# Four column tiles where sums or values run alone, and another order of the preparation

## The chip, the core and the metric

One core of one Trainium2 chip runs the whole program. The metric is the device time of one execution in microseconds (us), the median of several. The engines are TensorE (PE; its weight loads are PEld), VectorE (DVE), ScalarE (ACT), GpSimd (POOL) and SyncE (SP), which here issues every transfer. Each works through its own instructions in program order and waits on semaphores.

## The reference

Two layers of a gated decoder block on `x` and `ctx_1024`, both (8, 512, 256) in fp32. The first attention is the one that matters here:

```python
scores = jnp.einsum('bhqd,bhkd->bhqk', q, k) / math.sqrt(D_K)      # 16 heads, D_K = 16, S = 512
scores = jax.nn.softmax(scores, axis=-1)
col_sum = jnp.sum(scores, axis=2)                                  # how much each key is looked at
_, idx = jax.lax.top_k(col_sum, int(S * 0.9))                      # 460 of 512 keys stay
mask = zeros.at[..., idx].set(1.0)
out = jnp.einsum('bhqk,bhkd->bhqd', scores * mask[:, :, None, :], v)
```

Each part is added to the stream as `x + tanh(gate) * part(...)`. Behind this attention stand its output product, a feed-forward of width 704 with weights and inputs rounded to FP4 in blocks of 16, a second attention with a layer norm (without a softmax, so it becomes one 256x256 matrix per batch), and a linear layer rounded to 8 bits.

## The kernel before, in words

The work has three stages which share one program order per engine.

**Preparation** (`prepare`, `project`). SP loads weights and inputs in the order of `first`, `second` and `first_batch`. `project` makes for each batch the projections q, k, v (steps `Q0`, `Q1`, `K0`, `K1`, `V0`, `V1`), the transposes of the normalised x (`XT0`, `XT1`), and the matrix of the second attention (`GRAM`, `X1`, `RB`, `KV`, `MM`, `ROW`). `SEQ` lists these steps. The first 16 (`AHEAD`), up to `KV` of batch 1, run before the attention begins; the later ones are cut into pieces and put between the steps of the attention (`at_turn`, `ends_at`). q and k go out to HBM (`store_q`, `store_k`) and come back in another layout (`load` in `attend`, called `load_heads` in `run`). `stats(b)` takes the sums for the layer norm of x of batch b on DVE, `normal` applies it. `Fp4Weights` rounds the feed-forward's weights: `load` on SP, `maxima`, `scales`, `over` and `round` on DVE, `magnitude` on ACT, `split` on POOL, at the steps z of `LARGEST_AT` and `HALF_AT`.

**Attention** (`attend`). A unit u is half of the heads of a batch, 16 units, each of 16 steps z, 256 steps in all. In step z PE makes scores for two heads into `ps_a` (L1275), DVE takes their row maxima (`nmax`, L1356), ACT the exponentials into `ea` (L1442). `column_sums` (L1311) multiplies `ea` by the reciprocals of the row sums and adds up the keys' sums in `ps_s`; from its partitions 0 to 63 DVE ranks the keys of a unit (`rank_step`, from L1384) and marks the dropped ones. `LAG` = 42 steps later the scores are made again, with the mask and the softmax's shift as further rows of the product, into `ps_b`, ACT makes `prob` (L1458, and in the last steps L1455 head by head), and `values` (L1325) adds up the outputs in partitions 64 to 127 of `ps_s`, which DVE copies to `att` after every 8 steps (`leave`, L1408). Sums and values are products with 32 output columns, so one takes a strip of 32 columns of PE's array. A step has two heads of sums (strips 0 and 1) and two heads of values (strips 2 and 3):

```python
            for h in range(2):
                e.matmul(ps_s[32 * h:32 * h + 32, :], ...)            # column_sums, L1311
            for h in range(2):
                o = SUMS + 32 * h
                e.matmul(ps_s[o:o + 32, :], ...)                      # values, L1325
```

The trace counts each fp32 product as two matmuls. Values begin at z = 46 and end at z = 301, sums run from z = 4 to z = 259: before and after that one of the two is alone, on two strips.

**Feed** (`feed`). 16 units of 256 tokens go through output product (`first_product`, L1701), FP4 feed-forward (`gate_or_up`, L1728), second attention and 8-bit layer. Its first turns stand between the last 46 steps of the attention: `first_product` after steps 262, 268 and 284, `x_T` after 273 and 286, `gate_or_up` after the steps 275 to 282 and 288 to 295.

Of the kernel before, what the change touches and what calls it, by code (L numbers as in the profile page):

```python
# [9 lines left out]
F16 = mybir.dt.float16  # L10
# [65 lines left out]
CONST, CLEARED, ZEROED = 6, 8, 10  # L76
# [129 lines left out]
def prepare(m, a, w, ey, tiles, bank):  # L206
# [11 lines left out]
    def sync(e):  # L218
# [16 lines left out]
        def first():  # L235
# [26 lines left out]
    def gpsimd(e):  # L262
# [11 lines left out]
        e.tensor_copy(w.ident16[:, :], w.ident[:, :]).then_inc(w.s_set, 1)  # L274

# [26 lines left out]
    def vector(e):  # L302
# [46 lines left out]
        return bias_scale, bias_operand, round_w8, gated, scale_w8  # L349
# [7 lines left out]
class Fp4Weights:  # L357
# [37 lines left out]
    def load(self, e):  # L395
        a, w = self.a, self.w
        e.wait_ge(w.s_set, CLEARED)
        for n, name in enumerate(["L0_ffn_w_gate", "L0_ffn_w_up"]):
            e.dma_start(self.gn[:, n * FC:n * FC + FC - 1],
                        a[name][0:(FC - 1) * P].rearrange("(c p) i -> p c i", p=P)).then_inc(self.s_load, 16)  # L400
            e.dma_start(self.gn[0:FL, n * FC + FC - 1], a[name][(FC - 1) * P:F]).then_inc(self.s_load, 16)
        e.dma_start(self.dn[:, :, :], a["L0_ffn_w_down"].rearrange("(c p) i -> p c i", p=P)).then_inc(self.s_load, 16)
# [121 lines left out]
LARGEST_AT, HALF_AT = (0, 9, 18), (2, 6, 11, 15, 20, 24)  # L524


def project(m, a, w, ey, scr, bank, fp4):
# [100 lines left out]
    def sync(e):  # L628
# [245 lines left out]
    def vector(e):  # L874
# [32 lines left out]
        def fill(s):  # L907
# [186 lines left out]
def attend(m, w, scr, tiles, fp4):  # L1094
# [22 lines left out]

    APART = ALL_Z - LAG
# [9 lines left out]
    rank, top = m.sb("rank", [SUMS, T]), m.sb("top", [SUMS, 8])  # L1128
    drop = m.two("drop", [SUMS, T], F16)
# [34 lines left out]
    def sync(e):  # L1164
# [107 lines left out]
    def tensor(e):  # L1272
# [29 lines left out]
        def column_sums(g, k):  # L1302
# [1240 lines left out]
```

## Time and profile before

| | |
|---|---|
| median of 3 runs | 1188.7 us (1186.08 to 1189.09) |
| the profiled execution | 1184.63 us, its span 1182.9 us |
| PE busy | 1075.4 us, 91% of the span |
| DVE busy | 993.3 us, 84% |
| ACT busy | 905.6 us, 77% |
| POOL busy | 303.1 us, 26% |
| mean granted clock of PE | 0.971 |

Busy shares are means over the three stages and have to be read stage by stage: the preparation fills the first 45 us, the attention goes on until about 790 us, the feed alone until the end. The profiled execution took 1.7 us outside its span, and its own time is 0.3% under the median of the runs.

### The profile page before, as it was taken

To read this page: it belongs to the slowest core of one execution; us is meant where nothing else is said; L and a number is where in the kernel's file an instruction comes from. 1 tells how busy PE (TensorE), PEld (TensorE's weight loads), DVE (VectorE), ACT (ScalarE), POOL (GpSimd) and SP (SyncE) were. 2 spreads that over 40 slices of the span, in tenths; PEclk is the share of its full clock that TensorE was granted. 3 is DMA by queue.
4 is the path that set the end of the run, shared out by engine and by line. 5 is a ranking of instruction groups with operands and counts; after the bars stand their busy time and mean duration, and the time that the engine had idled before them with its cause. 6 is when DMAs were issued, how large, how long until landed. Compare 5 with 4: busy or idle time off the path is not lost.

```text
span 1182.9 us, 17878 instructions
## 1 busy us (share of the span) xinstructions
PE 1075.4 (91%) x5580; PEld 479.5 (41%) x5580; DVE 993.3 (84%) x1906; ACT 905.6 (77%) x2044; POOL 303.1 (26%) x473
## 2 busy tenths in 40 slices
PE   7697999999999999999998779999999999999975
PEld 4232232222232222232232113336677777777653
DVE  7599999789889889888789867357999999999965
ACT  4366799999989999999898985764677667667634
POOL 7264431221222222312211212002222212222212
PEclk9798999999999999999999989999999999999985
DMA  9712133134313222331322011001012111210001
GB/s 301 163 65 66 41 91 96 45 87 99 70 50 108 76 70 64 100 86 38 86 65 48 21 51 55 10 14 58 27 37 63 43 39 37 63 45 19 21 17 36
DMA packets 75966, 75.98 MB, mean 64 GB/s; under 512 B 11560, under 2 KB 67680, under 8 KB 75872
## 3 DMA queue, kind: packets, MB, share of 16 engines
q1 hardware_dynamic: 75872, 74.84, 23.0%
q8 instruction: 45, 0.74, 0.3%
q14 instruction: 49, 0.40, 0.1%
HBM read 47.02 MB, written 27.28 MB: 63 GB/s over the span
## 4 chain that ended last, share of the span: by engine, by line
PE 55%; ACT 20%; DVE 16%; issue 7%; DMA 1%; SPq 1%; POOL 0%; DVEq 0%; ACTq 0%
PE ps_a L1728 13%; ACT ea L1442 10%; PE ps_b L1686 8%; PE ps_s L1311 8%; ACT prob L1458 6%; DVE nmax L1356 6%; PE ps_s L1325 4%; PE ps_s L1686 3%; PE ps_b L1275 3%; PE ps_f L1701 2%; PE ps_f L831 2%; PE ps_a L1737 2%; PE ps_a L1275 2%; PE ps_f L802 2%; PE ps_f L1762 1%
## 5 line engine op out<-in xcount | busy, mean ns | idle before, releaser
L1442 ACT ACTIVATE ea<-ps_a,nmax 128x512 f32<-128x512 f32 x512 | 357.1, 726 | 65.9 <-DVE nmax L1356 64.6
L1356 DVE TENSOR_REDUCE nmax<-ps_a 128x2 f32<-128x1024 f32 x256 | 311.4, 1217 | 48.3 <-PE ps_a L1275 45.9
L1311 PE MATMUL ps_s<-ea,rz 128*32 128x512 f32 x1024 | 275.5, 617 | 19.9 <-DVE rank L1384 12.6
L1325 PE MATMUL ps_s<-prob,v_pad 128*32 128x512 f32 x1024 | 271.8, 610 | 4.3 <-DVE att L1408 3.5
L1458 ACT ACTIVATE prob<-ps_b 128x1024 f32<-128x1024 f32 x214 | 230.1, 1075 | 4.6 <-PE ps_b L1275 3.8
L1728 PE MATMUL ps_a<-wgu,xT 128*128 128x352 f32 x512 | 165.4, 463 | 3.3 <-ACT xT L1891 2.1
L1275 PE MATMUL ps_b<-q_st,k_st 52*128 52x512 f16 x512 | 102.8, 384 | 28.7 <-ACT prob L1458 26.5
L1442 ACT ACTIVATION_READ_ACCUMULATOR ea<-ps_a,nmax 128x1 f32 x512 | 125.2, 245 | 0.0
L1728 PEld LDWEIGHTS ps_a<-wgu,xT 128*128 128x128 f32 x512 | 92.4, 190 | 57.9 <-issue 14.5
L1275 PE MATMUL ps_a<-k_st,q_st 48*128 48x512 f16 x512 | 100.9, 390 | 5.5 <-ACT ea L1442 5.3
L1903 ACT ACTIVATE ea<-ps_a 128x352 f32<-128x352 f32 x128 | 59.5, 466 | 59.2 <-PE ps_a L1728 59.0
L1686 PE MATMUL ps_b<-wdn,hT 128*128 128x256 f32 (+1 forms) x384 | 94.9, 392 | 0.0
L1275 PEld LDWEIGHTS ps_a<-k_st,q_st 48*128 48x128 f16 x512 | 24.7, 93 | 147.3 <-ACT ea L1442 78.3
L1311 PEld LDWEIGHTS ps_s<-ea,rz 128*32 128x32 f32 x1024 | 37.6, 109 | 104.6 <-issue 91.5
L1686 PEld LDWEIGHTS ps_b<-wdn,hT 128*128 128x128 f32 (+1 forms) x384 | 67.6, 189 | 22.5 <-issue 15.9
L1395 DVE MATCH_REPLACE8 rank<-top,rank 64x512 f32<-64x512 f32 x112 | 74.8, 668 | 0.1
L1389 DVE MAX8 top<-rank 64x8 f32<-64x512 f32 x112 | 73.5, 656 | 0.2
L1455 ACT ACTIVATE prob<-ps_b 128x512 f32<-128x512 f32 x84 | 45.6, 597 | 32.4 <-PE ps_b L1275 32.3
L1275 PEld LDWEIGHTS ps_b<-q_st,k_st 52*128 52x128 f16 x512 | 26.5, 94 | 84.0 <-ACT prob L1458 46.5
L1629 POOL TENSOR_TENSOR x_in<-x_in,rows 128x512 f32<-128x512 f32 x16 | 20.4, 1272 | 118.8 <-DVE r L2067 103.6
L1325 PEld LDWEIGHTS ps_s<-prob,v_pad 128*32 128x32 f32 x1024 | 38.1, 108 | 28.6 <-issue 25.1
L1629 POOL TENSOR_TENSOR rb<-r,rows 128x512 f32<-128x512 f32 x16 | 21.2, 1323 | 103.1 <-DVE r L2206 103.1
(261 smaller groups left out, 1775.8 us busy)
## 6 DMA issues: line engine op xcount, KB each, us to landing
k_scr<-k_p SPq DMA_DIRECT2D x24, 256.0 KB, 3.0
q_scr<-q_p SPq DMA_DIRECT2D x24, 256.0 KB, 3.0
q_st<-q_scr SPq DMA_DIRECT2D x32, 192.0 KB, 4.9
k_st<-k_scr SPq DMA_DIRECT2D x32, 192.0 KB, 5.2
cT<-in_ctx_T SPq DMA_DIRECT2D x8, 512.0 KB, 5.6
x_in<-in_x SPq DMA_DIRECT2D x8, 512.0 KB, 7.8
c_in<-in_ctx SPq DMA_DIRECT2D x8, 512.0 KB, 5.5
v_scr<-v_s SPq DMA_DIRECT2D x8, 512.0 KB, 4.3
```

The source lines that it names most:

```text
L1275: return e.matmul(bank, left[b][o:o + rows, r, t * P:t * P + P], right[b][o:o + rows, r], start=True, stop=True)
L1311: e.matmul(ps_s[32 * h:32 * h + 32, :], rz[:, t, r, 2 * k + h, o:o + 32], ea[g % RING][:, 2 * k + h], start=(n == 0 and k == 0), stop=(n = ...
L1325: e.matmul(ps_s[o:o + 32, :], v_pad[u % 2][:, t, 4 * r + 2 * k + h], at.prob[g % PROBS][:, 2 * k + h], start=(t == 0 and k == 0), stop=(t ...
L1356: e.tensor_reduce(nmax[u % 2][:, t].rearrange("p (h r) -> p r h", h=2)[:, r], ps_a[:, z % 2 * 2:z % 2 * 2 + 2], AX_X, ALU.max, negate=True ...
L1389: e.max(top[:, :], rank[:, :]).then_inc(*dv.up())
L1395: e.match_replace(rank[:, :], top[:, :], rank[:, :], NEG).then_inc(*dv.up())
L1442: e.activation(ea[c % RING][:, g % 4], ps_a[:, g % 4], ACT.Exp, bias=nmax[u % 2][:, t, n:n + 1], accum_out=tot[u % 2][:, t, n:n + 1]).then ...
L1455: e.activation(dst[:, h], ps_b[:, h], ACT.Exp).then_inc(done, 1)
L1458: e.activation(dst, ps_b[:, :, :], ACT.Exp).then_inc(s_prob, 1)
L1686: ins = e.matmul(dst[t], left(c, t), right(c), start=(first and c == chunks[0]), stop=(last and (apart or t == N - 1) and c == chunks[-1]))
L1728: ins = e.matmul(gu[:, q % 2, 0:HALF_F], xT[:, c, t * P:t * P + P], w.wgu[:, c, k * HALF_F:(k + 1) * HALF_F], start=(c == 0), stop=(c == D ...
L1903: e.activation(dst[:, t, k % 2 * HALF_F:(k % 2 + 1) * HALF_F], gu[:, q % 2, 0:HALF_F], func).then_inc(s_act_gu, 1)
```

## The change

1. `column_sums` of units 0 and 1 (`SUMS_APART` = 2), while no values run, issues both pairs of heads of a group in one step, on all four strips of 32 columns, and nothing in the next step. The rank of these units works on 128 partitions, and the dropped keys are placed by four transfers instead of two.
2. `values` of the half-units from 27 on (`VALUES_APART` = 27, steps 262 to 301) does the same; `leave` copies 128 partitions there, and `store` issues four transfers instead of two.
3. SP: the row `BV1` and x of batch 1 are loaded earlier; x of batch 2 stands ahead of the store of q of batch 0 and of the FP4 weights, the read back of the first unit's q and k ahead of the FP4 weights too, which now come behind.
4. DVE: `stats` and `variances` of later batches stand at `RB` and `Q0` instead of `XT1`, `X1` and `RB`, those of batch 1 at `XT0`; the gating of the rows of biases goes to POOL, at step 32; `scale_w8` stands one step later; the FP4 work stands at other steps.

```diff
@@ prepare, sync: first
             row(BV, "L0_xattn_bv", ey.s_rows)
+            row(BV1, "L1_xattn_bv", ey.s_rows)
+            inputs_of(1)
             tokens_of(0)
-            inputs_of(1)
             weight(WK1)
             weight(WV1)
-            row(BV1, "L1_xattn_bv", ey.s_rows)
...
-LARGEST_AT, HALF_AT = (0, 9, 18), (2, 6, 11, 15, 20, 24)
+LARGEST_AT, HALF_AT = (2, 10, 18), (4, 8, 12, 16, 20, 24)
...
-        def first_batch(fp4):
+        def first_batch(fp4, load_heads):
             store_k(0)
             store_v(0)
             load_cT(1)
-            fp4.load(e)
+            load_x(2)
             store_q(0)
+            load_heads(0)
             load_c(1)
-            load_x(2)
+            for part in range(3):
+                fp4.load(e, part)
+            load_heads(1)
...
-            elif n == V1:
+            elif n == XT0:
                 stats(1, 0, TT)
                 variances(1)
...
             if 0 < b < B - 1:
-                if k == XT1:
+                if k == RB:
                     stats(b + 1, 0, 2)
-                elif k == X1:
+                elif k == Q0:
                     stats(b + 1, 2, TT)
-                elif k == RB:
                     variances(b + 1)
...
+    SUMS_APART, VALUES_APART = 2, 27
...
+            apart = u < SUMS_APART
+            o = FIRST_ROW - (r if apart else 2 * r + k)
             for h in range(2):
-                e.matmul(ps_s[32 * h:32 * h + 32, :], rz[:, t, r, 2 * k + h, o:o + 32], ea[g % RING][:, 2 * k + h],
-                         start=(n == 0 and k == 0), stop=(n == GROUPS - 1 and k == 1)).then_inc(s_colsum, 1)
+                q = 32 * h + (SUMS * k if apart else 0)
+                e.matmul(ps_s[q:q + 32, :], rz[:, t, r, 2 * k + h, o:o + 32], ea[g % RING][:, 2 * k + h],
+                         start=(n == 0 and (apart or k == 0)),
+                         stop=(n == GROUPS - 1 and (apart or k == 1))).then_inc(s_colsum, 1)
...
             for h in range(2):
-                o = SUMS + 32 * h
+                o = 32 * h + (0 if apart and k else SUMS)
                 e.matmul(ps_s[o:o + 32, :], v_pad[u % 2][:, t, 4 * r + 2 * k + h], at.prob[g % PROBS][:, 2 * k + h],
...
+        def both(z, apart):
+
+            if apart:
+                return () if z % 2 else (0, 1)
+            return (z % 2,)
...
             g = within((z - 4) // 2, ALL_G)
             if g is not None:
-                column_sums(g, z % 2)
+                for k in both(z, g // GROUPS < SUMS_APART):
+                    column_sums(g, k)
             g = within((z - LAG - 4) // 2, ALL_G)
             if g is not None:
-                values(g, z % 2)
+                for k in both(z, g // TT >= VALUES_APART):
+                    values(g, k)
...
-            load_heads(0)
-            load_heads(1)
...
+                if z == 32:
+                    gated()
...
-                if n == Q1:
-                    gated()
-                if n == FILLS + X1:
+                if n == FILLS + RB:
                     scale_w8()
```

The instructions of DVE just ahead of the attention, from the filling of `c1w` for batch 0 on (`rows<-rows,gate` is the gating, `st<-x_in` the statistics of x of batch 2, `x<-rows,c,ps_f` the step `X1`, `rb` the step `RB`), stand before as:

```order
L1005 TENSOR_SCALAR c1w<-ones,c 128x128 x2
L338 TENSOR_SCALAR rows<-rows,gate 128x256
L339 TENSOR_SCALAR rows<-rows,gate 128x512
L340 TENSOR_SCALAR rows<-rows,gate 128x256
L881 BN_STATS st<-x_in 128x6 x4
L943 SCALAR_TENSOR_TENSOR x<-rows,c,ps_f 128x256 x2
L344 TENSOR_SCALAR rows<-ps_a,gate 128x256
L346 TENSOR_TENSOR w<-ps_a,rows 128x512
L887 BN_AGGR mv<-st 128x2 x4
L889 TENSOR_SCALAR ve<-mv 128x4
L948 SCALAR_TENSOR_TENSOR rb<-rows,ps_b 128x256
```

and with the change as:

```order
L1013 TENSOR_SCALAR c1w<-ones,c 128x128 x2
L951 SCALAR_TENSOR_TENSOR x<-rows,c,ps_f 128x256 x2
L890 BN_STATS st<-x_in 128x6 x2
L956 SCALAR_TENSOR_TENSOR rb<-rows,ps_b 128x256
L347 TENSOR_SCALAR rows<-ps_a,gate 128x256
L349 TENSOR_TENSOR w<-ps_a,rows 128x512
L890 BN_STATS st<-x_in 128x6 x2
L896 BN_AGGR mv<-st 128x2 x4
L898 TENSOR_SCALAR ve<-mv 128x4
```

The copy of `X1` no longer stands behind the statistics of batch 2, and the gating has left DVE.

PE's instructions in the last steps of the attention, from step 272 to the second `gate_or_up` (`ps_b<-q_st,k_st` are the second scores, `ps_s<-prob,v_pad` the values, `ps_a<-ident,xg` is `x_T`, `ps_a<-wgu,xT` a quarter of `gate_or_up`), stand before as:

```order
L1325 MATMUL ps_s<-prob,v_pad 32x512 x2
L1708 MATMUL ps_a<-ident,xg 128x128 x4
L1275 MATMUL ps_b<-q_st,k_st 128x512 x2
L1325 MATMUL ps_s<-prob,v_pad 32x512 x2
L1275 MATMUL ps_b<-q_st,k_st 128x512 x2
L1325 MATMUL ps_s<-prob,v_pad 32x512 x2
L1728 MATMUL ps_a<-wgu,xT 128x352 x2
L1275 MATMUL ps_b<-q_st,k_st 128x512 x2
L1325 MATMUL ps_s<-prob,v_pad 32x512 x2
L1728 MATMUL ps_a<-wgu,xT 128x352 x2
```

and with the change as:

```order
L1362 MATMUL ps_s<-prob,v_pad 32x512 x4
L1304 MATMUL ps_b<-q_st,k_st 128x512 x2
L1757 MATMUL ps_a<-ident,xg 128x128 x4
L1304 MATMUL ps_b<-q_st,k_st 128x512 x2
L1362 MATMUL ps_s<-prob,v_pad 32x512 x4
L1304 MATMUL ps_b<-q_st,k_st 128x512 x2
L1777 MATMUL ps_a<-wgu,xT 128x352 x2
L1304 MATMUL ps_b<-q_st,k_st 128x512 x2
L1362 MATMUL ps_s<-prob,v_pad 32x512 x4
L1777 MATMUL ps_a<-wgu,xT 128x352 x2
```

The values of two steps stand together in the even one, four products in a row, each on a strip of its own.

## Rows read from the trace of the kernel before

**Rows 1.** The page: busy time of each engine, share of the span, instructions.

```profile
PE 1075.4 (91%) x5580; PEld 479.5 (41%) x5580; DVE 993.3 (84%) x1906; ACT 905.6 (77%) x2044; POOL 303.1 (26%) x473
```

**Rows 2.** Windows: length, busy us of PE, PEld, DVE, ACT, POOL; clock, DMA share, GB/s.

```profile
45.90:142.00 96.10, 82.77 (x323) 27.10 (x322) 86.48 (x145) 63.11 (x166) 48.73 (x68) 0.91 0.22 63
250.00:350.00 100.00, 93.30 (x578) 27.68 (x574) 87.28 (x163) 92.96 (x205) 24.61 (x55) 1.00 0.29 74
709.40:734.70 25.30, 24.31 (x103) 7.38 (x103) 20.12 (x53) 16.25 (x32) 6.24 (x7) 1.00 0.22 64
734.70:756.20 21.50, 21.50 (x83) 7.36 (x81) 5.12 (x16) 12.59 (x27) 1.02 (x1) 1.00 0.02 7
756.20:767.60 11.40, 9.93 (x44) 3.29 (x42) 6.93 (x7) 10.06 (x16) 0.00 (x0) 1.00 0.04 14
767.60:789.10 21.50, 21.50 (x82) 7.34 (x80) 11.03 (x26) 13.39 (x27) 1.01 (x1) 1.00 0.02 6
```

**Rows 3.** Timeline from 15 to 45 us: start, duration, instruction, [idle before and releaser].

```profile
15.15 0.69 DVE L970 TENSOR_TENSOR v_s<-ps_f,rows 128x512 f32<-128x512 f32 x1 [2.65 <-DMA rows<-in_L_xattn_bv]
...
26.07 0.37 SPq L645 DMA_DIRECT2D q_scr<-q_p  x1
...
28.75 1.43 SPq L631 DMA_DIRECT2D x_in<-in_x  x1
...
35.08 0.60 SPq L1176 DMA_DIRECT2D k_st<-k_scr  x1
...
37.04 1.41 DVE L881 BATCH_NORM_STATS2 st<-x_in 128x6 f32<-128x256 f32 x4 [8.69 <-DMA x_in<-in_x]
...
39.27 1.22 PE L864 MATMUL ps_f<-xT,wt 128*128 128x512 f32 x1 [6.72 <-DVE x L943]
...
44.69 0.55 PE L1275 MATMUL ps_a<-k_st,q_st 48*128 48x512 f16 x2
```

**Rows 4.** Transfers issued in the first 60 us: count, KB, median us to landing.

```profile
q_st<-q_scr SPq DMA_DIRECT2D x4, 192.0 KB, 6.1
dn<-in_L_ffn_w_down SPq DMA_DIRECT2D x1, 704.0 KB, 7.5
```

**Rows 5.** Waits of DVE from 45.9 to 142 us: total, times, longest.

```profile
DVE nmax L1356 <- PE ps_a L1275: 4.7, 6, 2.2
DVE m_sums L974 <- PE ps_b L851: 2.8, 1, 2.8
```

**Rows 6.** Timeline of PE, one step with sums and values.

```profile
663.82 0.62 PE L1311 MATMUL ps_s<-ea,rz 128*32 128x512 f32 x2
663.83 0.62 PE L1325 MATMUL ps_s<-prob,v_pad 128*32 128x512 f32 x2
...
664.84 0.39 PE L1275 MATMUL ps_a<-k_st,q_st 48*128 48x512 f16 x2
```

**Rows 7.** Timeline of PE, one step with values alone and a quarter of `gate_or_up`.

```profile
741.75 1.05 PE L1325 MATMUL ps_s<-prob,v_pad 128*32 128x512 f32 x4
742.74 1.45 PE L1728 MATMUL ps_a<-wgu,xT 128*128 128x352 f32 x4
```

**Rows 8.** Timeline from 714 to 732 us: ACT, DVE and PE ahead of `x_T`.

```profile
714.11 1.08 ACT L1455 ACTIVATE prob<-ps_b 128x512 f32<-128x512 f32 x2 [0.28 <-PE ps_b L1275]
...
720.56 0.69 DVE L2118 TENSOR_REDUCE xs<-xn 128x32 f32<-128x512 f32 x1 [1.55 <-ACT xn L1854]
...
724.28 0.69 DVE L1408 COPY att<-ps_s 64x512 f32<-64x512 f32 x1 [1.71 <-PE ps_s L1325]
...
731.17 0.66 PE L1708 MATMUL ps_a<-ident,xg 128*128 128x128 f32 x4 [0.64 <-DVE xg L2139]
```

**Rows 9.** Timeline of ACT at the attention's end.

```profile
794.92 0.60 ACT L1914 ACTIVATE hT<-ps_a 128x512 f32<-128x512 f32 x1 [1.01 <-PE ps_a L1737]
```

**Rows 10.** Timeline of PE where its clock falls and comes back.

```profile
697.27 0.61 PE L1275 MATMUL ps_b<-q_st,k_st 52*128 52x512 f16 x2 [1.86 <-ACT prob L1458]
...
704.50 0.62 PE L1311 MATMUL ps_s<-ea,rz 128*32 128x512 f32 x2
```

More of the change, by code:

```diff
@@ L274, in gpsimd, with gated @@
         e.tensor_copy(w.ident16[:, :], w.ident[:, :]).then_inc(w.s_set, 1)
+        def gated():
+            e.wait_ge(s_gate, 1)
+            e.wait_ge(ey.s_rows2, 64)
+            e.tensor_scalar(w.rows[:, BO], w.rows[:, BO], w.gate[:, 0:1], None, ALU.mult).then_inc(w.s_set, 1)
+            e.tensor_scalar(w.rows[:, GAM:BET + 1], w.rows[:, GAM:BET + 1], w.gate[:, 1:2], None,
+                            ALU.mult).then_inc(w.s_set, 1)
+            e.tensor_scalar(w.rows[:, B8], w.rows[:, B8], w.gate[:, 3:4], None, ALU.mult).then_inc(w.s_set, 1)
+        return gated
     def tensor(e):
@@ L393, in third, with load @@
         return x, k * FC * D // FB, nb, self.mag[k % 2][:, 0:nb * FB].rearrange("p (n d) -> p n d", d=FB)
-    def load(self, e):
+    def load(self, e, part):
         a, w = self.a, self.w
+        if part == 2:
+            e.dma_start(self.dn[:, :, :],
+                        a["L0_ffn_w_down"].rearrange("(c p) i -> p c i", p=P)).then_inc(self.s_load, 16)
+            return
         e.wait_ge(w.s_set, CLEARED)
[L398 to L402, printed above, removed]
+        x = a["L0_ffn_w_up" if part else "L0_ffn_w_gate"]
+        e.dma_start(self.gn[:, part * FC:part * FC + FC - 1],
+                    x[0:(FC - 1) * P].rearrange("(c p) i -> p c i", p=P)).then_inc(self.s_load, 16)
+        e.dma_start(self.gn[0:FL, part * FC + FC - 1], x[(FC - 1) * P:F]).then_inc(self.s_load, 16)
     def maxima(self, e, k):
@@ L1127, in attend @@
     SUMS = P // 2
-    rank, top = m.sb("rank", [SUMS, T]), m.sb("top", [SUMS, 8])
-    drop = m.two("drop", [SUMS, T], F16)
+    rank, top = m.sb("rank", [P, T]), m.sb("top", [P, 8])
+    drop = m.two("drop", [P, T], F16)
     ps_a = m.ps("ps_a", [P, 4, 512])
@@ L1158, in half, with placed, stored @@
         return u, k // 2 % TT, k // (2 * TT) * 2 + k % 2
+    def placed(u):
+        return DROPS * (u // BUFS + 1 + (u % BUFS < SUMS_APART))
+    def stored(n):
+        return sum(64 if k >= VALUES_APART else 32 for k in range(n % 2, n + 1, 2))
     def starts(z, at):
@@ L1196, in place_dropped @@
                 o = 64 * h + KA + NSHIFT
-                e.dma_start(k_st[u % BUFS][o:o + 1], drop[u % 2][32 * h:32 * h + 4]).then_inc(s_ld[u % BUFS], 16)
+                dst = k_st[u % BUFS][o:o + 1]
+                if u >= SUMS_APART:
+                    e.dma_start(dst, drop[u % 2][32 * h:32 * h + 4]).then_inc(s_ld[u % BUFS], 16)
+                    continue
+                for k in range(2):
+                    q = SUMS * k + 32 * h
+                    e.dma_start(dst.rearrange("n (r k) t -> n r k t", k=2)[:, :, k],
+                                drop[u % 2][q:q + 2]).then_inc(s_ld[u % BUFS], 16)
         def store(u, r):
@@ L1203, in store @@
                 o = SUMS + 32 * h
-                e.dma_start(rows[h], att[r][o:o + 32]).then_inc(s_lo[r], 16)
+                if 2 * u + r < VALUES_APART:
+                    e.dma_start(rows[h], att[r][o:o + 32]).then_inc(s_lo[r], 16)
+                    continue
+                for k, q in ((0, o), (1, 32 * h + DK)):
+                    e.dma_start(rows[h][k], att[r][q:q + DK]).then_inc(s_lo[r], 16)
         def step(z):
@@ L1378, in rank_step @@
         def rank_step(u, n):
+            rows = slice(0, P if u < SUMS_APART else SUMS)
             if n == 0:
@@ L1383, in rank_step @@
                     e.wait_ge(s_drop, u)
-                e.tensor_scalar(rank[:, :], ps_s[0:SUMS, ::-1], -1.0, None, ALU.mult).then_inc(s_rank, 1)
+                e.tensor_scalar(rank[rows, :], ps_s[rows, ::-1], -1.0, None, ALU.mult).then_inc(s_rank, 1)
                 e.wait_ge(s_rank, u + 1)
@@ L1406, in leave @@
             if n >= 2:
-                e.wait_ge(s_lo[n % 2], 32 * (n // 2))
-            e.tensor_copy(att[n % 2][SUMS:P, :], ps_s[SUMS:P, :]).then_inc(s_att, 1)
+                e.wait_ge(s_lo[n % 2], stored(n - 2))
+            rows = slice(0 if n >= VALUES_APART else SUMS, P)
+            e.tensor_copy(att[n % 2][rows, :], ps_s[rows, :]).then_inc(s_att, 1)
         def step(z):
```

44 lines of the change are left out of this document (23 added, 21 removed).

## The prediction

> **What bounds the kernel now.** I read first the page's busy times, which name PE (91%) but average three stages [rows 1], then windows by stage, then the timelines at the places where the change acts. In the middle of the attention, from 250 to 350 us, ACT is busy 92.96 of 100 us and PE 93.30 [rows 2]; there the change touches nothing but the place of some statistics on DVE, so these some 550 us stay. The change acts at three places:
>
> - *Ahead of the attention.* DVE stands idle for 8.69 us until x of batch 2 lands, which SP issued only at 28.75 us; behind these statistics stands the copy that PE waits for (6.72 us), and the first scores come at 44.69 us [rows 3].
> - *Units 0 and 1*, from 45.9 to about 142 us. DVE is busy 86.48 of 96.1 us, PE 82.77 at a mean clock of 0.91 [rows 2]. DVE's largest waits for PE are 4.7 and 2.8 us [rows 5]: DVE bounds this stretch, PE only in part.
> - *Steps 262 to 301*, from about 709.4 to 794 us. In both stretches with `gate_or_up` (734.7 to 756.2 and 767.6 to 789.1) PE is busy all of 21.50 us while ACT has 12.59 and 13.39 [rows 2]. Here PE is the bound. In the other two parts PE shares it with a chain of the feed through DVE and ACT, below.
>
> **The price of the four strips.** A step with sums and values runs four products on four strips: from 663.82 to the next instruction at 664.84, 1.02 us [rows 6]. A step with values alone runs two products on two strips: from 741.75 to 742.74, 0.99 us [rows 7] (each product counts as two in the trace). So twice as many products cost nearly the same. The change turns two steps of 0.99 us into one of 1.02 and one of nothing: 1.98 - 1.02 = 0.96 us of PE saved in two steps.
>
> **Steps 262 to 301.** *With `gate_or_up`*: 8 steps each, 4 pairs of steps, 3.8 us off each 21.5 us, 7.7 us together. ACT would then have its 13.4 us in 17.7 us, so PE stays the bound. *Steps 262 to 274*: PE would save 6.2 us, but it already waits 0.64 us for DVE before `x_T`, and DVE had waited on the way 1.55 us for ACT and 1.71 us for the values [rows 8]. The second goes and part of the first; the rest of the chain (DVE busy 20.12 of 25.3 us [rows 2]) remains. Bounds 0 and 3.9 us (the three waits together), I take 2.3. *Steps 283 to 287*: ACT has 10.06 us of 11.4 [rows 2]; bounds 0 and 1.3, I take 0.7. *The end*: in the last four steps two groups of four take the place of four pairs, 1.9 us less of PE, and ACT waits 1.01 us for what follows them [rows 9]; that wait goes, and then ACT is late; I take 1.0. The copy of `leave` grows from 64 to 128 partitions: it took 0.69 us [rows 8], and the nearest copy-like instruction from PSUM with 128x512, `v_s`, took 0.69 too [rows 3], so it costs nothing. The ten more stores lie behind no one. Sum 7.7 + 2.3 + 0.7 + 1.0 = 11.7 us.
>
> With two strips more in use, the emptying side should show itself first where nothing else fills PE: ACT needs 1.08 us a step and waits 0.28 for PE [rows 8], so a step without `gate_or_up` can't come below 1.08 us, which is why I cut 6.2 to 2.3. The Trainium skill ("TensorEngine Tiling (Array Packing)", section "PSUM Bottleneck") says that tiling speeds up TensorE but not the emptying of PSUM, which may become the limit. By that rule the steps without `gate_or_up` could give no more than ACT's waits, 13 x 0.28 = 3.6 us and not PE's 6.2, and the trace agrees; for those with `gate_or_up`, where ACT is busy for 12.59 of 21.50 us, the trace says otherwise, and there the sum goes by PE.
>
> **Units 0 and 1.** PE saves 16 times 0.96 = 15.4 us, but only what DVE loses by waiting for PE counts: 4.7 + 2.8 us [rows 5] and 1 us of small ones. A part of that is the turn from unit 0 to 1, where PE waits for the rank and DVE for PE after it; this stays. Bounds 0 and 8.5, I take 3.0. The rank on 128 partitions costs as `leave` does: nothing.
>
> **Ahead of the attention.** x of batch 2 is issued behind cT, at about 20 us instead of 28.75 (an estimate: the FP4 loads, `store_q` and c stood between). It took 37.04 - 28.75 = 8.3 us to land, so it lands at 28.5 us, while its statistics stand behind `X1` now. PE's 6.72 us of idle time go, and the row `BV1`, for which DVE waited 2.65 us [rows 3], comes earlier and pulls q of batch 0 forward by about as much. PE alone could start at about 44.7 - 6.7 - 2.7 = 35.3 us. But the first unit's q and k must be back: `store_q` stood at 26.07 [rows 3], now at 23.4; from it to the end of the four issues that read back it took until 35.08 + 0.60 [rows 3], 9.6 us, and the landing 6.1 us [rows 4]: 39.1 us with as much traffic as before, and 36 with the FP4 loads gone from in front. I take 37.7: 7 us earlier. The price is the FP4 loads behind it. They start at some 32 us, issue for 4 us, the last lands 7.5 us later [rows 4], at about 43.5; DVE asks for them in step 2, some 4.3 us after the start, at 42. A wait of 0 to 3 us, I take 1.0. What remains is 6.0 us, with bounds 2 and 10. The gating on DVE (three instructions) lay in the wait for x and frees nothing; on POOL, busy 48.73 of 96.1 us [rows 2], it is hidden.
>
> **The clock.** After a wait of 1.86 us a pair of scores takes 0.61 us instead of 0.39 (1.2 instead of 2.4 GHz), and the sums have their 0.62 us back at 704.50 [rows 6, 10]: some 7 us at half speed, 3.5 us of PE's work. The change makes PE idle more both in units 0 and 1 and before `x_T`. On the other hand the long idle time before 39.27 goes. I charge 1.5 us, bounds -2 and 6.
>
> **Sum.** 11.7 + 3.0 + 6.0 - 1.5 = 19.2 us from the profiled execution's own 1184.63: 1165.4. That execution is 0.34% under the median of the runs, so the median should be 1165.4 x 1188.7 / 1184.63 = 1169.4; I say **1169**. About 0.3%, 3.6 us, is what a measurement of this kernel can tell from no change.
>
> **The rivals.**
> 1. *The head gives nothing* (1175 us, 0.14). The FP4 loads or the read back of q and k come so late that DVE's wait only moves from `X1` to step 0 or 2. For it: transfers fill the first 35 us and move along when one goes ahead. Against it: nothing is added to them. The 6.0 us fall away.
> 2. *The feed's chain holds the tail* (1174 us, 0.10): with shorter steps `x_T` and the gates wait for DVE, POOL and ACT, and of 11.7 us some 6.5 remain. For it: the 0.64 us before `x_T`; against it: DVE is busy only 5.12 of 21.5 us in the first gate stretch.
> 3. *All bounds on the good side* (1158 us, 0.14): head 9, units 0 and 1 8.5, tail 13.5, no clock lost, 31 us.
> 4. *Four products of one kind don't run beside each other as two and two do* (1183 us, 0.05): the strips give nothing and the head's 6 us remain. Against it: [rows 6] show four at once, sums and values two each.
> 5. *Slower: PE's clock stays at 1.2 GHz in the tail* (1204 us, 0.07). With less work per step the clock falls before `x_T` and doesn't come back. The work in both gate stretches is 2 x 17.7 = 35.4 us at full clock, 70.8 at half, against 43.0 now: 27.8 us lost, 9 + 4 gained elsewhere, 15 slower. It decides from about 42 us at half clock on, since each such us loses half a us and 21 are gained. Against it: the fall at 697 us ended after 7 us, and from 756.2 to 767.6 PE was busy 9.93 of 11.4 us at full clock. The Trainium skill ("TensorE: Matmul & The Clock Gate", section "The HAM clock gate") says that the throttled state is the default and activity releases it: the same mechanism, and the trace agrees in that busy stretches show 1.00.
>
> My forecast has 0.50, alone from 1163 to 1175. **The range**: the lowest tenth lies in rival 3, the highest in rivals 4 and 5, so 1157 to 1180. Faster by over 0.3%: everything but rival 5 and a weak tail of 4, 0.91; within 0.3%: 0.03; slower: 0.06.
>
> **What would show it.** First scores at 36 to 39 us instead of 44.69, no DVE idle time before `X1`'s copy; a wait of `maxima` for its load of at most 3 us. Four products of sums or of values in a row with the next instruction 1.0 us behind. About 3 us less between z = 0 and unit 2's first sums. Gate stretches of 17.7 us instead of 21.5, `x_T` about 2 us sooner after step 262. The feed alone, from 803 us, unchanged in length. Wrong would be: 1.9 us for such four, a half clock in the gate stretches, or a middle of the attention that changes by more than 3 us, since I count nothing for the moved statistics.

## The result, and the profile after

The changed kernel takes 1174.96 us (median of 4 runs, 1172.92 to 1175.31), the kernel before 1188.58 us beside it (4 runs, 1186.08 to 1189.09). The ratio is 0.9895, 95% interval 0.9869 to 0.9921: faster by 13.6 us. The forecast was 1169 with a range of 1157 to 1180.

The profiled execution took 1175.31 us (span 1173.6), the slowest of its four, while that of before was quick for its kernel; between the two spans lie only 9.3 us, and the place by place account below divides these 9.3. The page of the changed kernel begins:

```profile
PE 1050.4 (90%) x5580; PEld 476.9 (41%) x5580; DVE 990.2 (84%) x1903; ACT 905.0 (77%) x2044; POOL 304.8 (26%) x476
```

PE lost 25 us of work beside [rows 1], and the time fell by 9. The same stretches as in [rows 2], with the same columns (length, busy us of PE, PEld, DVE, ACT, POOL, granted clock, DMA), now lie here:

```profile
38.50:139.70 101.20, 74.12 (x324) 27.46 (x324) 86.23 (x144) 63.71 (x168) 51.90 (x72) 0.83 0.34 92
250.00:350.00 100.00, 93.07 (x572) 27.56 (x570) 87.46 (x164) 92.62 (x205) 24.63 (x55) 1.00 0.27 73
702.20:729.47 27.27, 22.60 (x102) 7.69 (x103) 20.27 (x54) 15.41 (x30) 6.25 (x7) 0.81 0.20 59
729.47:747.15 17.68, 17.68 (x82) 6.82 (x80) 4.13 (x13) 12.55 (x26) 1.02 (x1) 1.00 0.04 9
747.15:761.08 13.93, 10.05 (x46) 3.24 (x46) 7.93 (x9) 12.07 (x18) 0.00 (x0) 0.83 0.05 11
761.08:778.76 17.68, 17.68 (x80) 7.22 (x80) 10.55 (x25) 11.34 (x24) 1.01 (x1) 0.94 0.04 8
```

Units 0 and 1 take 101.2 us, with 8.7 us less PE work and a lower clock. The window of before ends 0.6 us short of the same step; from the first maxima of step 0 to those of step 36 it is 96.7 us before and 101.3 now. Both stretches with `gate_or_up` take 17.68 us instead of 21.50, and the stretches around them take longer than before: 27.3 against 25.3 us, and 13.9 against 11.4. The second 17.68 is no second 3.82 us saved: this window holds only three groups of four products (the fourth starts at 778.70 us) and 1.0 us of half clock. From its start to that of the scores of step 297 it is 21.49 us before, 18.61 here and 17.61 in e5 below.

The timeline of the head, SP, DVE and PE (start, duration, instruction, idle time and releaser), shows what takes the place of the waits in [rows 3]:

```profile
27.07 1.43 SPq L651 DMA_DIRECT2D q_scr<-q_p  x3
...
32.78 0.60 SPq L1194 DMA_DIRECT2D k_st<-k_scr  x1
...
31.32 0.87 DVE L951 SCALAR_TENSOR_TENSOR x<-rows,c,ps_f 128x256 f32<-128x256 f32 x2 [7.81 <-PE ps_f L802]
...
38.04 0.39 PE L1304 MATMUL ps_a<-k_st,q_st 48*128 48x512 f16 x2 [1.57 <-DMA k_st<-k_scr]
...
45.89 1.75 DVE L413 TENSOR_REDUCE fs<-gn 128x96 f32<-128x1536 f32 x1 [2.79 <-DMA dn<-in_L_ffn_w_down]
```

DVE no longer waits for x of batch 2, its 8.69 us; PE starts the scores at 38.04 us instead of 44.69 and waits for the read back of k. The first maxima wait 2.79 us for the last FP4 load.

PE in a pair of steps with `gate_or_up`, and in the last two steps before its clock falls (x8: four products, two entries each):

```profile
731.17 1.07 PE L1362 MATMUL ps_s<-prob,v_pad 128*32 128x512 f32 x8
732.17 1.45 PE L1777 MATMUL ps_a<-wgu,xT 128*128 128x352 f32 x4
733.55 0.39 PE L1304 MATMUL ps_b<-q_st,k_st 52*128 52x512 f16 x2
733.87 1.45 PE L1777 MATMUL ps_a<-wgu,xT 128*128 128x352 f32 x4
735.26 0.39 PE L1304 MATMUL ps_b<-q_st,k_st 52*128 52x512 f16 x2
735.58 1.06 PE L1362 MATMUL ps_s<-prob,v_pad 128*32 128x512 f32 x8
```

```profile
708.00 0.39 PE L1304 MATMUL ps_b<-q_st,k_st 52*128 52x512 f16 x2
709.17 0.79 PE L1304 MATMUL ps_b<-q_st,k_st 52*128 52x512 f16 x2 [0.78 <-ACT prob L1503]
709.88 1.06 PE L1362 MATMUL ps_s<-prob,v_pad 128*32 128x512 f32 x8
710.88 0.39 PE L1304 MATMUL ps_b<-q_st,k_st 52*128 52x512 f16 x2
711.96 1.09 PE L1304 MATMUL ps_b<-q_st,k_st 52*128 52x512 f16 x2 [0.69 <-ACT prob L1503]
712.98 1.93 PE L1362 MATMUL ps_s<-prob,v_pad 128*32 128x512 f32 x8
```

Four products on four strips take 1.00 us (731.17 to 732.17), a pair of steps 4.41 us (731.17 to 735.58). Without `gate_or_up` a pair of steps takes 2.88 us (708.00 to 710.88) and PE idles in it. At 711.96 the clock falls from 2.4 to 1.2 GHz: the two scores there take 1.09 us instead of 0.79, and the four products 1.93 instead of 1.06.

Of the 9.3 us, by the starts of the same steps in both traces (up to step 255 the first maxima on DVE, behind it the second scores on PE): 7.4 are there at z = 0; units 0 and 1 give 4.6 back (2.8 at z = 36); 4.4 come until step 262 (7.2 there); 2.2 in steps 262 to 297 (9.4 there). Behind them 1.1 us come until the next `gate_or_up` (13.46 us from step 297 instead of 14.59) and stand through the feed; 1.2 are lost in the program's last 45 us, where PE's clock lies differently (0.50 in the last 7.9 us, 0.71 before).

### The profile page after: what moved, and what is told of

The parts are those of the page before. It is cut to its first block, busy times and chain, and to the rows that moved or that the text cites. A ratio compares the mean times of both kernels' runs of the same rounds, so it can differ in the third digit from the quotient of the medians.

```text
span 1173.6 us, 17894 instructions
## 1 busy us (share of the span) xinstructions
PE 1050.4 (90%) x5580; PEld 476.9 (41%) x5580; DVE 990.2 (84%) x1903; ACT 905.0 (77%) x2044; POOL 304.8 (26%) x476
## 4 chain that ended last, share of the span: by engine, by line
PE 54%; ACT 21%; DVE 15%; issue 6%; DMA 1%; POOL 1%; SPq 1%; DVEq 0%; ACTq 0%
PE ps_a L1777 13%; ACT ea L1490 10%; PE ps_b L1735 8%; PE ps_s L1342 7%; ACT prob L1506 7%; DVE nmax L1402 6%; PE ps_s L1362 3%; PE ps_b L1304 3%; PE ps_s L1735 3%; PE ps_f L1750 2%; PE ps_a L1786 2%; PE ps_a L1304 2%; PE ps_f L811 2%; PE ps_f L840 2%; PE ps_f L1811 2%
## 5 line engine op out<-in xcount | busy, mean ns | idle before, releaser
L1342 PE MATMUL ps_s<-ea,rz 128*32 128x512 f32 x1024 | 258.5, 625 | 31.4 <-DVE rz L1413 16.6
L1362 PE MATMUL ps_s<-prob,v_pad 128*32 128x512 f32 x1024 | 252.8, 617 | 4.6 <-DVE att L1456 2.8
L1304 PE MATMUL ps_b<-q_st,k_st 52*128 52x512 f16 x512 | 104.2, 386 | 32.9 <-ACT prob L1506 24.6
L1342 PEld LDWEIGHTS ps_s<-ea,rz 128*32 128x32 f32 x1024 | 35.5, 109 | 112.9 <-issue 89.3
L1442 DVE MATCH_REPLACE8 rank<-top,rank 64x512 f32<-64x512 f32 (+1 forms) x112 | 74.9, 669 | 0.0
L1436 DVE MAX8 top<-rank 64x8 f32<-64x512 f32 (+1 forms) x112 | 73.7, 658 | 0.2
L2179 DVE SCALAR_TENSOR_TENSOR ea<-ea 128x512 f32<-128x512 f32 (+1 forms) x32 | 36.0, 1126 | 11.9 <-ACT ea L1931 7.2
```

The costliest lines, as they stand in the source:

```text
L1304: return e.matmul(bank, left[b][o:o + rows, r, t * P:t * P + P], right[b][o:o + rows, r], start=True, stop=True)
L1342: e.matmul(ps_s[q:q + 32, :], rz[:, t, r, 2 * k + h, o:o + 32], ea[g % RING][:, 2 * k + h], start=(n == 0 and (apart or k == 0)), stop=(n ...
L1362: e.matmul(ps_s[o:o + 32, :], v_pad[u % 2][:, t, 4 * r + 2 * k + h], at.prob[g % PROBS][:, 2 * k + h], start=(t == 0 and (apart or k == 0) ...
L1436: e.max(top[rows, :], rank[rows, :]).then_inc(*dv.up())
L1442: e.match_replace(rank[rows, :], top[rows, :], rank[rows, :], NEG).then_inc(*dv.up())
```

## The experiments

"New preparation" is all of the change but the strips. Kernels of one chip shared their runs of before. Ratios are to before on the same chip; they are estimated with their interval from all runs and differ by up to 0.0007 from the quotient of the medians. Step times are of one profiled execution each.

| run | kernel | chip | median us | before | ratio, 95% |
|---|---|---|---|---|---|
| e1 | new preparation | A | 1177.18 | 1184.46 | 0.9944 (0.9922 to 0.9966) |
| e2 | e1 + values on four strips | A | 1171.58 | 1184.46 | 0.9887 (0.9866 to 0.9908) |
| e3 | e1 + sums on four strips | A | 1179.27 | 1184.46 | 0.9956 (0.9938 to 0.9974) |
| e4 | before + both strips | A | 1181.41 | 1184.46 | 0.9967 (0.9951 to 0.9984) |
| e5 | e2, FP4 steps earlier | B | 1167.12 | 1183.34 | 0.9868 (0.9845 to 0.9891) |
| e6 | e5, first maxima a step later | B | 1167.79 | 1183.34 | 0.9875 (0.9860 to 0.9890) |
| e7 | e5, values on four from step 270 | B | 1169.84 | 1183.34 | 0.9887 (0.9872 to 0.9902) |
| e8 | e5 + extra matmuls in the tail | B | 1168.81 | 1183.34 | 0.9880 (0.9865 to 0.9895) |
| e9 | e5 again | C | 1166.90 | 1183.84 | 0.9855 (0.9839 to 0.9871) |
| e10 | e9 + sums on four strips | C | 1171.69 | 1183.84 | 0.9892 (0.9879 to 0.9905) |
| e11 | e10 + extra matmuls | C | 1170.45 | 1183.84 | 0.9894 (0.9873 to 0.9916) |
| e12 | before + order of loads, FP4 steps of e5 | C | 1175.48 | 1183.84 | 0.9927 (0.9913 to 0.9941) |

### e1 to e4: which part gives what

e1 is the kernel before with all hunks but the strips', e4 with the strips' alone. e2 and e3 are the changed kernel with

```diff
-SUMS_APART, VALUES_APART = 2, 27
+SUMS_APART, VALUES_APART = 0, 27    # e2
+SUMS_APART, VALUES_APART = 2, 32    # e3
```

> The new order of the preparation alone, sums and values on two strips as before. Theory A (the head's gain of about 7 us at step 0 is kept, and the sums on four strips throw half of it away, because PE, less busy in units 0 and 1, has its clock lowered): step 36 some 6 us earlier than before, time about 6 us under before, 0.995. Theory B (the later FP4 work and the moved statistics cost it, the strips are innocent): step 36 only 2 to 3 us earlier, time 0.998.

> The whole change without the four strips for the sums of units 0 and 1. Theory A: about 3 us faster than the changed kernel, 1172 us, ratio to before 0.986. Theory B: the sums gave a little, so 1 to 3 us slower than the changed kernel, 0.991.

> The whole change without the four strips for the values. Both theories: the values gained 2 to 3 us from step 262 on by the trace, so 1177 us, ratio 0.991; if the trace's 3 us of shift in the middle is a matter of clock luck, up to 1180.

> Four strips for sums and values, the preparation as before. Theory A: the sums cost 0 to 3 us, the values give 2 to 3: 1186 to 1190, 1.000. Theory B: sums and values give 5 us together: 1183, 0.996.

The values on four strips give 0.0057 (e1 to e2) and 0.0061 (e3 to the changed kernel), some 7 us (the changed kernel was run apart from them, beside its own runs of before). The preparation alone gives 7.3 us by the medians, 6.6 by the ratio. The sums on four strips give nothing: +0.0012 from e1 to e3, +0.0008 from e2 to the changed kernel, neither beyond the intervals. e4, both strips beside the old preparation, gives 0.0033, some 4 us, less than the values alone give beside the new one; its first stretch of the tail took 28.6 us, and the mean clock of its runs is 0.958 to 0.968. From z = 0 to z = 36 the traces show 96.7 us before, 100.8 in e1, 102.0 in e2, 100.6 in e3 and 97.3 in e4: so units 0 and 1 became longer by the new preparation and not by the strips, as theory B had it. The times don't decide between the two so clearly: 0.994 for e1 is theory A's number (its head gained 9.5 us at z = 0), 0.997 for e4 is theory B's, 0.989 for e2 lies between them. In e2 PE stands still at its first turn for the FP4 weights. Its row, and that of the GpSimd instruction it waits for:

```profile
74.09 1.09 PE L485 MATMUL ps_b<-ident,gn 128*128 128x128 f32 x4 [1.68 <-POOL gn L465]
75.11 0.61 PE L1304 MATMUL ps_a<-k_st,q_st 48*128 48x512 f16 x2
75.65 1.84 PE L1342 MATMUL ps_s<-ea,rz 128*32 128x512 f32 x4
```

```profile
70.16 0.99 POOL L463 TENSOR_TENSOR gn<-fm,gn 128x384 f32<-128x384 f32 x1 [0.90 <-DVE gn L451]
71.23 0.84 POOL L465 TENSOR_TENSOR gn<-gn,fs 128x384 f32<-128x384 f32 x1
72.03 1.00 POOL L463 TENSOR_TENSOR gn<-fm,gn 128x384 f32<-128x384 f32 x1
73.11 0.84 POOL L465 TENSOR_TENSOR gn<-gn,fs 128x384 f32<-128x384 f32 x1
```

The second half of `gn` is written at 73.95 us, because `HALF_AT` starts this half at step 8 instead of 6; POOL itself had waited for DVE's rounding. PE then goes on at half its clock, and the maxima for the next step are late.

### e5 and e6: the FP4 steps

```diff
-LARGEST_AT, HALF_AT = (2, 10, 18), (4, 8, 12, 16, 20, 24)
+LARGEST_AT, HALF_AT = (2, 9, 18), (3, 6, 11, 15, 20, 24)
```

> The kernel of e2 (new preparation, values on four strips, sums on two) with the FP4 preparation back at its old steps but for the first maxima: maxima at steps 2, 9, 18 and halves at 3, 6, 11, 15, 20, 24 (e2: 2, 10, 18 and 4, 8, 12, 16, 20, 24). Theory A (in units 0 and 1 the later halves cost: PE stands before its first two FP4 turns until GpSimd has written the second half of gn, 1.7 us of it seen at the first turn and 1.7 us before the column sums ahead of it, and then runs at half clock): the 3 us of steps 10 to 16 come back, z=0 to z=36 takes 98 to 99 us instead of 102, the run is 2.5 to 4 us below e2 (about 1168). Theory B (the time is lost to the FP4 loads, to DVE's moved statistics, or to a clock that falls with any idle time): no change against e2, within 1 us.

e6 has `(3, 9, 18), (4, 7, 11, 15, 20, 24)`.

> As e5, but the first maxima at step 3 and halves at 4, 7, 11, 15, 20, 24: DVE's first maxima no longer wait for the down projection's load (1.8 to 2.8 us in e1 and in the changed kernel), but the second half is split at step 10, one step later than in e5. If the wait for the load is the other part of the loss: 1 to 2.5 us below e5, the gap from step 2 to step 4 shrinks from 7 to 5 us. If the load is only the last of several waits there (DVE is also ahead of PE at that place): within 1 us of e5.

PE's turn in e5:

```profile
70.20 1.05 PE L1342 MATMUL ps_s<-ea,rz 128*32 128x512 f32 x4 [1.14 <-DVE rz L1413]
71.19 0.66 PE L485 MATMUL ps_b<-ident,gn 128*128 128x128 f32 x4
```

No wait for POOL, no fall of the clock; z = 0 to z = 36 takes 97.9 us instead of 102.0, as theory A said. The changed kernel shows the same wait at a smaller size, 0.80 us for POOL and then the half clock. The profiled spans differ by 5.5 us, the ratios of e2 and e5 by 0.0019 (2 us; other chip, and the intervals overlap), of e2 and e9 by 0.0032 (also other chip, and the intervals overlap a little). In e6 DVE's wait before step 4 goes (step 2 to 4 takes 5.4 us instead of 8.1), but z = 0 to 36 takes 99.4 us: the later second half costs more than the wait. The medians of e5 and e6 lie 0.7 us apart, within the intervals: the wait for the load is not worth a step.

### e7 and e8: the tail and PE's clock

e7 has `SUMS_APART, VALUES_APART = 0, 28`.

> As e5, but the values go to four strips from half unit 28 (step 270) instead of 27 (step 262). In steps 262 to 269 no gate or up product fills PE, two steps take 2.88 us with pairs and with quads alike, and PE idles more with quads. If the idle time brings PE's clock down at steps 268 to 274 (seen at 712 us in the changed kernel, 4 us lost) the later start avoids it: 0 to 3 us below e5, and the granted clock of 705 to 725 us after is 1.0. If the fall there is not tied to the quads: within 0.7 us of e5.

e8, ahead of the second head's score in the even steps:

```diff
+if h and (z + LAG) % 2 == 0 and (262 <= z + LAG <= 274 or 284 <= z + LAG <= 290):
+    for o in range(0, 4 * P, P):
+        e.matmul(ps_a[:, 3, o:o + P], w.ident16[:, :], w.ident16[:, :], start=True, stop=True)
```

> As e5, with four matmuls of 128x128 (bf16, into a bank that nobody reads then) ahead of the second score in the even steps 262 to 274 and 284 to 290, where PE otherwise waits 0.69 us for ACT's prob. Clock theory of the tail (PE's idle time brings its clock down and the steps then take twice as long in products that PE bounds): the granted clock in the tail is 1.0, and the run 2 to 5 us below e5, or below the mean of the kernels whose clock fell. Rival (the handshake PE to ACT to PE bounds these steps and the clock's fall costs little): equal to e5 or up to 1.5 us slower by the extra matmuls' time.

Of e5, the windows of the same four stretches as above:

```profile
698.46:721.77 23.31, 18.44 (x102) 6.26 (x102) 19.27 (x51) 15.46 (x31) 5.81 (x7) 1.00 0.24 69
721.77:739.45 17.68, 17.68 (x80) 6.81 (x80) 5.03 (x16) 12.39 (x26) 1.46 (x2) 1.00 0.04 8
739.45:753.35 13.90, 9.92 (x47) 3.40 (x46) 7.93 (x9) 10.99 (x18) 0.00 (x0) 0.88 0.05 11
753.35:771.05 17.70, 17.70 (x85) 6.91 (x81) 10.69 (x25) 13.34 (x27) 1.01 (x1) 1.00 0.04 8
```

Of e8, the first and the third:

```profile
700.30:724.54 24.24, 19.91 (x128) 7.55 (x127) 19.46 (x51) 15.91 (x30) 5.98 (x7) 1.00 0.22 67
742.20:754.90 12.70, 9.19 (x60) 3.76 (x58) 7.94 (x9) 11.24 (x18) 0.00 (x0) 1.00 0.06 13
```

And of e12 (below), whose values stand in pairs as before, the third:

```profile
748.81:761.82 13.01, 11.54 (x45) 3.68 (x43) 7.10 (x7) 10.12 (x17) 0.00 (x0) 0.87 0.04 12
```

*First stretch.* With the clock at 1.00 it takes 23.3 us, with a mean of 0.81 it takes 27.3 (the changed kernel), and 27.07 in the profile of e9, whose kernel is that of e5. e8's extra matmuls make it 24.2 us at 1.00.

*Third stretch.* With the values in pairs it takes 11.4 us before, at 1.00, and 13.0 us in e12 at 0.87, from the same instructions (e3 13.0 us and e1 12.7, both at 0.87): the fall of the clock costs 1.3 to 1.6 us there. With four strips it takes 13.9 us at 0.88 (e5) and at 0.83 (the changed kernel), and 12.7 at 1.00 in e8 even with extra matmuls in it. So of the 2.5 us by which it is longer in the changed kernel, some 1.6 are the clock's, which falls there in the pair kernels too, and 0.9 (13.9 against 13.0 in e12) come with the four strips.

e8 didn't test what it was built for: PE's wait (0.69 us, as before) is ahead of the even step's first score, so the extra matmuls stand behind it and not in it, and make a pair of steps 3.04 us long. Its run is 1.7 us above e5, within the intervals. e7 is 2.7 us above e5 where I expected it below, also within the intervals. Its first stretch took 24.6 us at 0.97, and its clock stood at half from 747.5 to about 758 us. As e5's profile has no fall in the first stretch either, the two don't show whether a fall there is tied to the four products.

The 0.9 us of the third stretch are a wait for ACT. The changed kernel's ACT there, its PE, and PE before:

```profile
749.62 1.28 ACT L1957 ACT_TABLE_LOAD   x1
750.92 1.38 ACT L1957 ACTIVATE ea<-ea 128x1408 f32<-128x1408 f32 x1
752.31 1.28 ACT L1503 ACT_TABLE_LOAD   x1
753.60 2.22 ACT L1503 ACTIVATE prob<-ps_b 128x512 f32<-128x512 f32 x4
```

```profile
751.56 0.39 PE L1304 MATMUL ps_b<-q_st,k_st 52*128 52x512 f16 x2
754.25 0.88 PE L1304 MATMUL ps_b<-q_st,k_st 52*128 52x512 f16 x2 [2.30 <-ACT prob L1503]
```

```profile
762.39 0.88 PE L1275 MATMUL ps_b<-q_st,k_st 52*128 52x512 f16 x2 [1.36 <-ACT prob L1455]
```

`gate(0)` puts 3.94 us into ACT's order (two changes of table of 1.28 us each, and the function), before as now. PE, which reaches this place with less work left, waits 2.30 us instead of 1.36 (e12: 1.36): what two steps save on PE goes into this wait. The Trainium skill ("ScalarE: Activation LUTs", section "What ACT_TABLE_LOAD costs") gives about 1283 ns for the load, and the trace agrees; the 1380 ns drain that it adds for each change doesn't show here, the next ACTIVATE starts 1.29 us after the load did.

### e9 to e12: the sums again, and the loads alone

> The kernel of e5 once more, as the control for the three beside it on one chip: 0.9865 to 0.989 of before, z=0 to z=36 in 98 us, and, where PE's clock stays, steps 262 to 297 in 74 us.

e10 is e9 with `SUMS_APART = 2`, e11 with the extra matmuls of e8 besides.

> e5 with the column sums of units 0 and 1 on four strips too (all of the change, with the earlier FP4 steps). If the sums' strips are worth something once no FP4 turn holds PE (the forecast of the prediction, 3 us): 2 to 4 us below e9, z=0 to z=36 in 94 to 96 us. If DVE bounds units 0 and 1: z=0 to z=36 within 1 us of e9 and the same time. If the idle time that they leave on PE is paid for with its clock: 1 to 4 us slower than e9, with a lower mean clock from 60 to 140 us.

> e10 with the extra matmuls of e8 in the even steps 262 to 274 and 284 to 290. If the falls of PE's clock in the tail that the changed kernel showed (5 us between steps 268 and 290) come with its idle time there: the tail's clock stays at 1.0, steps 262 to 297 take 74 us, and the run is 2 to 5 us below e10 when e10's tail takes 77 to 79 us. If e10's tail takes 74 us as well, the fall is not tied to these steps, and e11 equals e10 or is 1 us slower.

e10 is 4.8 us slower than e9 on the same chip, and the intervals don't overlap: with the FP4 wait out of the way the sums on four strips cost. Units 0 and 1 in the profiles of e9 (first row) and e10 (second):

```profile
36.00:134.20 98.20, 82.47 (x324) 26.86 (x324) 87.21 (x144) 63.40 (x166) 52.83 (x71) 0.91 0.36 96
```

```profile
36.00:134.20 98.20, 75.27 (x324) 27.31 (x324) 87.08 (x145) 64.22 (x168) 52.06 (x71) 0.83 0.35 95
```

DVE has the same 87 us of work in both, and PE's 7 us less are worth 0.8 us (z = 0 to 36: 98.9 and 98.1 us). What changes is the clock, 0.83 for 0.91, and over the whole span 0.963 to 0.965 in all four runs of e10 against 0.972 to 0.976 in the five of e9. But this profile is the quickest run of e10 (1169.59) and that of e9 the second slowest (1170.12), so the two don't show where 4.8 us go. The profile of e11 (1175.14) shows one such place, the turn from unit 1 to 2. PE of e11, and then DVE:

```profile
134.51 0.39 PE L1304 MATMUL ps_a<-k_st,q_st 48*128 48x512 f16 x2 [1.24 <-ACT ea L1493]
136.11 1.92 PE L1345 MATMUL ps_s<-ea,rz 128*32 128x512 f32 x4 [1.21 <-DVE rank L1434]
137.96 2.08 PE L825 MATMUL ps_b<-cT,wt 128*128 128x512 f32 x2
139.97 0.61 PE L1304 MATMUL ps_a<-k_st,q_st 48*128 48x512 f16 x2
```

```profile
140.64 1.23 DVE L1405 TENSOR_REDUCE nmax<-ps_a 128x2 f32<-128x1024 f32 x1 [3.42 <-PE ps_a L1304]
```

PE waits twice, does the next 3.9 us of work at 1.2 GHz, and DVE stands idle for 3.42 us. In e10's profile the same instructions took 1.05 and 1.13 us, and DVE waited 1.39 us. In the tail e11's clock stayed at 1.00 until 750 us and then fell (0.65 from 750 to 760): from the second scores of step 262 to those of step 297 it took 78.0 us, against 78.3 in e10 and 73.4 in e5. Against e10 e11 shows no difference (0.9894 and 0.9892).

e12, beside the FP4 steps of e5 and the early `BV1` and x of batch 1, in `first_batch` of the kernel before:

```diff
             load_cT(1)
-            fp4.load(e)
+            load_x(2)
             store_q(0)
+            load_heads(0)
             load_c(1)
-            load_x(2)
+            for part in range(3):
+                fp4.load(e, part)
+            load_heads(1)
```

> Before with the order of the loads alone (second value bias and second batch's inputs ahead of the tokens, x of batch 2 before store_q, heads 0 before the context of batch 1, FP4 loads last) and the FP4 steps of e5; statistics, gated rows and the W8 scale stay where they were, no strips. If the loads give the head's gain alone: first scores at 37 to 40 us, 0.9925 to 0.994 of before. If the moved statistics of batch 1 or the W8 scale share in it: first scores at 41 to 44 us, 0.995 to 0.998.

The scores of e12 start at 38.20 us (38.04 in the changed kernel), PE's last wait is for `k_st` in both (2.11 and 1.57 us). So the loads alone bring the head's gain. Whether moved statistics, gated rows on POOL and the later W8 scale add something isn't decided: the first scores of the kernels with all of the new preparation lie from 35.5 to 38.1 us, in one profile each. e12 and e9 differ by the values' strips and these moves: 0.0072, 8.6 us.

## Why the prediction was right, and where its steps were off

The sum of 19.2 us was too large by 5.6 (13.6 measured), the direction and the mechanism of the two large terms right. Between the two profiles, to which the sum was made, it is only 9.3, and that the number came as near as it did was in part luck: 4.4 us in the middle, for which I had nothing, made up for units 0 and 1, forecast at 3.0 gained and 4.6 lost. Term by term, with the profile of the changed kernel:

- **Price of four strips**: right. 1.00 us for four products, 4.41 us for a pair of steps.
- **Stretches with `gate_or_up`, 7.7 us**: right, 21.50 to 17.68 and 17.70 us in e5, 7.6 us. The changed kernel has 3.8 us in the first; in the second 1.0 us goes to the half clock at its start (the first `gate_or_up` takes 2.45 us at 761.08 instead of 1.45).
- **Steps 262 to 274, 2.3 us**: 2.0 us in e5, and 2.0 us lost in the changed kernel, where the clock fell. A pair of steps takes 2.88 us with four products as with two pairs: they stand between the even step's scores and the odd step's, ACT gets nothing meanwhile, and PE then waits 0.69 to 0.78 us for ACT ahead of the next even step's scores. I had bounded this by the waits' sum and not by that loop.
- **Steps 283 to 287, 0.7 us**: wrong sign, 0.9 us lost at equal clock (13.9 in e5 against 13.0 in e12). I read ACT's 10.06 of 11.4 us [rows 2] as room for 1.3 us, but PE waited 1.36 us there already for ACT, behind the two table changes of `gate(0)`; less work ahead of that place makes the wait longer (2.30 us). The other 1.6 us by which the stretch grew are the clock's.
- **The end, 1.0 us**: came, 1.1 us from step 297 to the next `gate_or_up` in every profiled kernel with the values on four strips. The changed kernel and e5 lose it again in the last 45 us of the program, by the clock; e8 and e4 keep 1.1 and 0.9 of it.
- **Head, 7 us**: right in size, 7.4 us by the first maxima, 6.65 by the first scores. `store_q` stands at 27.07 us, not 23.4 (26.07 before; in e3, with the same preparation, at 23.45, and the scores at 36.27), and DVE's wait before `X1` did not vanish but is now for PE (7.81 us). Two moves were needed. Before, k was back at 41.66 us, while PE's chain behind x of batch 2 ended at 44.69; now that chain ends at 36.47 us and k is back at 37.91. So the earlier x gave the first 3.0 us, and the rest came from `load_heads(0)` ahead of the FP4 loads: its last issue starts at 32.78 us instead of 35.08 and lands after 5.1 us instead of 6.6. e12 shows that the loads alone do it.
- **FP4 wait, 1.0 us**: 2.79 us, within its bounds, and the smaller part of that matter: I had looked at the first maxima only. That `HALF_AT`'s second half stood two steps later, with PE's turn at its old place, I had not priced; e5 shows 4 us from z = 0 to 36 in the profiles and 2 to 4 us in the medians.
- **Units 0 and 1, 3.0 us**: failed. DVE's waits for PE were taken as time that less PE work gives back. They end at the loop of scores, maxima, sums and rank, not at PE's load: with 7 us less on PE e10 gained 0.8 us in its quickest run, and over its runs it lost 4.8.
- **Clock, 1.5 us**: too small. In the tail of the changed kernel it made 4.0 us in the first stretch (27.3 against 23.3), 1.2 to 1.6 in the third and 1.0 behind it, some 6.4 together, past my bound of 6; a fall that only the profile of before has gives 1.6 back (next point). It is also all that was found to set e10 apart from e9.
- **Middle, nothing**: 4.4 us came before step 262, more than the 3 us that I had called a failure. Some 1.6 of them are a fall of the clock that the profile of before has after the rank at 587.70 us and that of the changed kernel doesn't (at 589.56, L802 x4 takes 1.91 us); the profiles of e7, e11 and e12 have it too. Another 1.1 come in steps 256 to 262, and 1.1 in steps 55 to 60. The latter are there in all profiles with the new preparation and 0.1 in e12, without the moved statistics, but 1.0 also in e4, which lacks them too, so the cause is open. From z = 60 to z = 200 e1 and the changed kernel gain 0.5 us and e12 none: the moved statistics are worth no more than that there.

Of the rivals, none came. The nearest was the second, but what held the tail was the clock and the hand over between PE and ACT, not the feed's chain ahead of `x_T`. The fifth has its mechanism at a quarter of its size (some 6.4 of 27.8 us): the clock fell three times in the tail, for 3 to 7 us each, and came back each time.

e9, with both values on four strips and the new loads, the sums on two and the FP4 steps early, is the best of these kernels: 1166.9 us, 0.9855 of before and 4.8 us below e10, which is all of the change with the same FP4 steps. Against the changed kernel itself (0.9895) it was only compared through before.

What stays open: where e10's runs lose their 4.8 us in each execution (one place was seen, in e11), and whether matmuls that really fill PE's waits would hold its clock in the tail. e8's did not stand in the wait.

## What to carry to other kernels

Work taken from an engine pays where that engine is busy all of the stretch (17.68 of 17.68 us: all of the saving came), and not where it waits in a loop with others; there it may turn into idle time, and on PE into a lower clock. When a load is moved, follow the whole chain behind it to its last consumer on every engine: the FP4 loads' price was not in DVE's wait for them but two engines on, in PE's turn. Where a bound engine is relieved, look for the waits that it already has for others: they grow by what it saves (here 1.36 to 2.30 us for ACT). And before a stretch's length is put down to a mechanism, set it beside a kernel that lacks the change: the third stretch of the tail was 1.6 us longer in e12 too, by a fall of the clock alone.

## What the runs showed of the hardware

- The clock's falls are not the same from one execution to the next. e5 and e9 are one kernel: the profile of e5 (1166.49 us) has no fall in the first stretch of the tail and takes 23.3 us there, that of e9 (1170.12 us) has one and takes 27.1, and the spans differ by 3.6 us. The other runs of e9 lie at 1164.56, 1166.29 and 1166.90 us with a mean clock of 0.975 to 0.976, and at 1170.46 with 0.972. A profile therefore holds one draw, and stretches should be compared at equal clock. The Trainium skill ("TensorE: Matmul & The Clock Gate", section "What's actually happening") says of a kernel's start that the number of matmuls at the lower clock varies from run to run; here the runs show a variation in the midst of the program.
- Without such a fall at the turn from unit 1 to 2 DVE waited 1.39 us (e10), with it 3.42 us (e11): the fall costs at a place where another engine waits for PE. It costs too where PE itself waits for ACT: in the third stretch of the tail before and e12 run the same instructions, PE waits 1.36 us for ACT in both, and they take 11.4 us at 1.00 and 13.0 at 0.87.
- Groups of four fp32 products of 32 columns, on four strips, take 1.00 us, two such on two strips 0.99 [rows 7]: twice the products in the same time of PE.
